# One lookup field's rows fetched by SyncE for every second tile instead of every third, with its row numbers on the chip, and the first gram portions ahead of two lookups

## What is computed

```python
e = jnp.stack([tbl_0[ids[:, 0]], ..., tbl_31[ids[:, 31]]], axis=1)      # [2048, 32, 256]
dots = jnp.einsum('bnd,bmd->bnm', e, e)
z = dots[:, iu, ju]                                                    # 496 pairs, i < j
h = jnp.concatenate([z, dense_ctx], axis=1)                            # 512 features
h = jnp.maximum(h @ W_top1 + b_top1, 0.0)                              # 512 -> 512
h = jnp.maximum(h @ W_top2 + b_top2, 0.0)                              # 512 -> 256
y = h @ W_top3                                                         # 256 -> 1
```

## Time and profile before

| | us |
|---|---|
| median of 3 runs (549.89 to 554.2) | 552.4 |
| profiled execution, its own time | 549.18 |
| its span, first to last instruction | 547.4 |

### The profile page before, as it was taken

The page is one execution under the profiler, slowest core; times in us unless marked ns, Lnnn a source line. Parts: engine busy times, 40 slices in busy tenths (PEclk is TensorE's granted clock), DMA queues, the critical chain, the costliest instruction groups (busy, mean ns, idle before and its releaser), DMA issues.

```text
span 547.4 us, 26273 instructions
## 1 busy us (share of the span) xinstructions
PE 502.7 (92%) x11015; PEld 463.4 (85%) x11015; DVE 249.3 (46%) x592; ACT 184.0 (34%) x355; POOL 393.2 (72%) x421
## 2 busy tenths in 40 slices
PE   0765899999999999999999999999899999989997
PEld 0764898999999989899888989989799998988986
DVE  3675462543536263343626435362633536253132
ACT  1786160522406051240605124060511505051152
POOL 6777767777777777777777777777777777777710
PEclk9997999999999999999999999999999999999999
DMA  8999544444444444444445444444444443443310
GB/s 198 263 262 311 146 117 121 120 120 130 120 120 128 120 121 125 120 118 128 118 121 129 122 118 119 130 120 118 127 121 118 118 125 118 116 116 109 111 32 2
DMA packets 38515, 71.10 MB, mean 130 GB/s; under 512 B 10942, under 2 KB 24638, under 8 KB 38398
## 3 DMA queue, kind: packets, MB, share of 16 engines
q0 software_dynamic: 19872, 54.29, 35.6%
q1 hardware_dynamic: 18526, 15.14, 11.3%
HBM read 69.39 MB, written 0.01 MB: 127 GB/s over the span
## 4 chain that ended last, share of the span: by engine, by line
PE 59%; POOL 22%; issue 9%; DMA 7%; DVE 2%; ACT 1%; POOLq 0%; DVEq 0%
PE look_ps L382 23%; POOL rows L336 22%; PE quad_ps L404 12%; PE top_ps L463 7%; DMA rows<-in_tbl,row_ids 6%; PE quad_ps L366 5%; PE turn_ps L366 5%; PE top_ps L484 4%; PE quad_ps L425 1%; PE top_ps L448 1%; DVE turned L689 1%; PE turn_ps L463 1%; ACT area L578 0%; DVE one_hot L761 0%; PE turn_ps L484 0%
## 5 line engine op out<-in xcount | busy, mean ns | idle before, releaser
L336 POOL DMA_INDIRECT rows<-in_tbl,row_ids x414 | 392.4, 948 | 128.4 <-issue 115.5
L382 PE MATMUL look_ps<-one_hot,small 125*128 125x256 f32 (+1 forms) x1536 | 220.3, 292 | 6.4 <-DVE small L751 6.2
L382 PEld LDWEIGHTS look_ps<-one_hot,small 125*128 125x128 f32 x1536 | 194.6, 192 | 9.8 <-issue 7.2
L761 DVE TENSOR_SCALAR one_hot<-ids_across,sub_row 125x256 fp32r<-125x256 int32 (+1 forms) x384 | 117.7, 378 | 119.9 <-PE look_ps L382 114.2
L404 PE MATMUL quad_ps<-turned 128*32 128x31 f32 x7680 | 103.8, 199 | 3.5 <-issue 2.5
L404 PEld LDWEIGHTS quad_ps<-turned 128*32 128x32 f32 x7680 | 85.7, 110 | 23.4 <-issue 4.5
L557 ACT ACTIVATE ahead<-look_ps 128x512 f32<-128x512 f32 (+1 forms) x48 | 28.0, 584 | 200.8 <-PE look_ps L382 200.4
L366 PE MATMUL turn_ps<-ident,rows 128*128 128x128 f32 x418 | 63.1, 281 | 23.4 <-DMA rows<-in_tbl,row_ids 21.2
L366 PEld LDWEIGHTS turn_ps<-ident,rows 128*128 128x128 f32 x418 | 46.5, 142 | 28.5 <-issue 15.0
L366 PE MATMUL quad_ps<-ident,rows 128*128 128x128 f32 x410 | 61.9, 281 | 7.1 <-DMA rows<-in_tbl,row_ids 5.8
L548 ACT ACTIVATE turned<-turn_ps 128x512 f32<-128x512 f32 x57 | 36.2, 635 | 64.2 <-PE quad_ps L404 44.8
(11 more groups left out here) (68 smaller groups left out, 196.0 us busy)
## 6 DMA issues: line engine op xcount, KB each, us to landing
area<-in_tbl SPq DMA_DIRECT2D x640, 1.0 KB
rows<-in_tbl,row_ids POOLq DMA_INDIRECT x414
ids_across<-in_small_ids SPq DMA_DIRECT2D x45, 128.0 KB, 3.5
landed<-in_tbl SPq DMA_DIRECT2D x6, 896.0 KB
w_sb<-in_W_top SPq DMA_DIRECT2D x4, 256.0 KB
landed<-in_tbl SPq DMA_DIRECT2D x6, 104.0 KB
w_sb<-in_W_top SPq DMA_DIRECT2D x1, 512.0 KB
area<-in_dense_ctx SPq DMA_DIRECT2D x16, 8.0 KB
```

What stands on the lines that cost most here:

```text
L336: pool.indirect_dma_start(out=rows[:, n % PLACES, j, :], out_offset=None, in_=tables[f], in_offset=bass.IndirectOffsetOnAxis(ap=row_ids[:, ...
L382: last = pe.matmul(look_ps[:, c * width:(c + 1) * width], small[:, f, r, part, c * P:(c + 1) * P], one_hot[n % 2][:, r, 0:width], start=(r ...
L761: last = dve.tensor_scalar(one_hot[n % 2][:, r, 0:width], ids_across[0:SP, n % IDS_RING, 0:width], sub_row[:, r:r + 1], None, ALU.is_equal)
```

## The change

Three things are changed.

1. `ROW_TILES` is now 3, 5, 7, 9, 11, 13 and 15: SP fetches field 31 for seven tiles in place of five, and POOL issues 412 gathers in place of 414. The eight groups for a tile are spread over two steps of SP's loop, four a step, after the first, the second and (two) the third list of ids.
2. The row numbers of these tiles (14 rows of 64) are copied once into a buffer on the chip, `row_list_sb`, and a group loads its 16 registers from there. The list of ids number 5 is loaded earlier.
3. In step 0 the gram portions 0 to 3 go ahead of lookup 4, which then runs in one piece; lookup 5 is cut into the last four portions (`first_look`).

```diff
-    ROW_EVERY = 3
-    ROW_TILES = list(range(ROW_EVERY, TILES, ROW_EVERY))
+    ROW_EVERY = 2
+    ROW_TILES = list(range(3, TILES, ROW_EVERY))
     ROWS_AT_ONCE = 16
     ROW_GROUPS = P // ROWS_AT_ONCE
-    GROUPS_AFTER = 3
+    GROUPS_AFTER = [1, 1, 2]
+    LISTED = P // 2
...
+        row_list_sb = sbuf("row_list_sb", [2 * len(ROW_TILES), LISTED], int32)
...
             def fetch_rows(i, group):
-                t = ROW_TILES[i]
                 if group == 0 and i > 0:
                     sp.wait_ge(turn_done, BEGIN[ROW_TILES[i - 1]] + ROW_UNIT + 1)
-                at = t * P + group * ROWS_AT_ONCE
+                if group == 0 and i == 0:
+                    sp.wait_ge(row_list_in, 16)
+                half, at = divmod(group * ROWS_AT_ONCE, LISTED)
                 _, numbers = nc.values_load_multi_w_load_instructions(
-                    row_list[0:1, at:at + ROWS_AT_ONCE], engines=[mybir.EngineType.SP],
+                    row_list_sb[2 * i + half:2 * i + half + 1, at:at + ROWS_AT_ONCE], engines=[mybir.EngineType.SP],
...
+            load_ids(5)
+            sp.dma_start(row_list_sb[:, :], row_list).then_inc(row_list_in, 16)
             load_dense(0)
...
-            load_ids(5)
             for t in range(TILES):
                 made = range(FIRST[t + 1], FIRST[t + 2]) if t + 2 in FIRST else range(0)
-                for k in range(GROUPS_AFTER):
+                begin = ROW_TILES[0] - ROW_EVERY
+                group = (t - begin) % ROW_EVERY * sum(GROUPS_AFTER)
+                for k, groups in enumerate(GROUPS_AFTER):
                     if k < len(made):
                         load_ids(made[k])
-                    group = t % ROW_EVERY * GROUPS_AFTER + k
-                    if t < ROW_TILES[-1] and group < ROW_GROUPS:
-                        fetch_rows(t // ROW_EVERY, group)
+                    if begin <= t < ROW_TILES[-1]:
+                        for _ in range(groups):
+                            fetch_rows((t - begin) // ROW_EVERY, group)
+                            group += 1
...
+            def first_look(k):
+
+                fifth, sixth = FIRST[0], FIRST[0] + 1
+                if k == PARTS // 2:
+                    look_up(fifth, 0, PRODUCTS)
+                if k > PARTS // 2:
+                    at = k - PARTS // 2 - 1
+                    look_up(sixth, PRODUCTS * at // (PARTS // 2), PRODUCTS * (at + 1) // (PARTS // 2))
...
                 for k in range(PARTS):
-                    look_between(t, k)
+                    if t > 0:
+                        look_between(t, k)
+                    else:
+                        first_look(k)
...
-                look_between(t, PARTS)
+                if t > 0:
+                    look_between(t, PARTS)
+                else:
+                    first_look(PARTS)
...
-    laid["row_list"] = np.ascontiguousarray(by_slot[:, FIELDS - 1].reshape(1, BATCH))
+    laid["row_list"] = np.ascontiguousarray(by_slot[:, FIELDS - 1].reshape(TILES, P)[3::2].reshape(-1, P // 2))
```

More of the change, by code:

```diff
@@ L189, in dlrm_tower @@
         table_in = [sem(f"table_in{i}") for i in range(SMALL)]
+        row_list_in = sem("row_list_in")
         rows_in = [sem(f"rows_in{i}") for i in range(len(ROW_TILES))]
```

## The result

The changed kernel takes 582.9 us (median of 4 runs, 580.91 to 584.57), the kernel before 551.75 in the same comparison: 5.8% slower, ratio 1.0576 with an interval of 1.054 to 1.0612. The forecast was 548.5, the range ended at 582.

The account below looks back on a forecast made before the run. POOL's gathers were taken as the bound; two gathers fewer (2.5 us) and step 0's new order (1.4) gave 3.9 us, SP's queue costing nothing, so 548.5 us from a median of 552.4, range 544 to 582.

Parts of the forecast that it names:

- What bounds the kernel: Whole span: POOL, one gather every 1.25 us, is the bound; PE keeps just ahead at 31.4 us a step.
- Part 1, two gathers fewer: POOL's queue: 412 gathers in place of 414 gain 2.5 us, with POOL staying the bound.
- Part 2, step 0: Start: gram portions ahead of lookup 4 let POOL's late gather at 73.05 go on time; gain 1.4 us.
- Part 3, SP's queue: SP's fetch of 128 rows every second tile: it fits POOL's 63.9 us with 1.8 us of room, costing nothing.
- the term x: SP's queue before each group: time of one register load from the buffer on the chip, taken as 0.6 us.
- The limit of 0.82 us: SP's load from the chip: below this time SP costs nothing against POOL's 63.9 us for two tiles.
- the period 57.3 + 8x: SP's cycle between last turns of its tiles: 57.3 us of issues and small terms plus eight loads; forecast 62.1.
- the prediction's formula: Span if SP decides: 138 to tile 3's last turn, six periods, 22.4 to the end; 504.2 + 48x.
- the 5.0 that the rivals' prices add: Whole kernel: medians taken as span plus 5.0 us, from 552.4 - 547.4 of the kernel before.
- a little too slow: Rival on SP's loads: x from 0.82 to 1.5, median 557 at 1.0 and 581 at 1.5; chance 0.17.
- The rule of a price for each register: SP's loads: about 200 ns per register from HBM; if true on chip, x 3.2, period 82.9, span 673.
- The floor of about 0.6 us for a load: SP's loads: skill's floor of about 600 ns for a tensor_load, cited for x = 0.6 and the period 62.1.

Follow-up runs that it names:

- load_once: The changed kernel with one load of 16 row numbers at the start, reused for every group (wrong rows fetched); 547.1 us, ratio 0.9911 to the kernel before.
- hbm_two: The changed kernel with SP's registers loaded from the list in HBM again, two loads a group; 698.8 us in one run.

## Why the prediction was wrong

**What bounds the kernel**: right. With SP out of the way (load_once) the gain was 0.9% where 0.7% was forecast, and POOL's last gather started at 519.1.

**Part 1, two gathers fewer**: 2.5 us were counted, and load_once with its 547.1 allows that and the gain of step 0 together. In the changed kernel they were worth nothing, since POOL waited some 30 us for PE.

**Part 2, step 0**: the mechanism was half right. The wait at lookup 4 went, and 4.5 us of stands in the middle of portion 2 and lookup 4 came for it. The step counted with portions of 0.8 us back to back, and nothing in its rows showed that PE would run through them without a stand. The kernel before already had such a stand of 1.36 us at 62.83 in its step 0, which I left out. The part by itself gave 0.5% in runs, more than the 1.4 us counted (0.25%). That it gave more is luck as far as the working goes: it was counted from a start with a mild wait of 1.68 us, and other starts of the old order have over 5.

**Part 3, SP's queue**: the sum was right and the term x was wrong. The limit of 0.82 us, the period 57.3 + 8x, the place of the wait (the last unit of every second tile), what is behind it, all came out. The step that failed is the choice x = 0.6 for the load: it measured 1.37. I took the pair of loads from HBM as two equal trips, of which the chip spares the whole, and left almost nothing for the 16 numbers. The runs show that most of the 1.37, 16 x 0.057 = 0.9, is paid by the number.

The prediction says that the pair doesn't tell whether 16 numbers cost more than one address. The gap doesn't, but the trace of the kernel before does, in the two rows of line 285 above: 1.17 us for the address and 1.83 for the 16 numbers. The trips were not equal, and the longer list cost 0.66 us more. An estimate from these rows alone, that this 0.66 stays and that SP's steps around the loads (the gap of at least 3.4 less 1.17 and 1.83, 0.4) stay too, is x = 1.06 before anything for the access on the chip. That is over the limit of 0.82, and by the prediction's own price the change would have been forecast as a small loss.

The other terms that were off by less:

- With x = 1.37 the prediction's formula gives a span of 504.2 + 48 x 1.37 = 570.0; measured were 581.1, which is 11.1 more. Tile 3's last turn was put at 138, and ended at 144.99: the first fetch began at 77.32 and not at 70, as PE's step 1 was not earlier, and was already SP-bound. That is 7.0 us.
- The period was 68.75 (from 144.99 to tile 15's 557.48) in place of 68.26, six times 0.5 = 2.9 us. It is the turn of the last unit, put at 0.4: behind PE's wait it takes 0.63 to 1.09 us, 0.93 in the mean of the six. From the turn's end to SP's first row DMA it is 1.36 us (144.99 to 146.35), the load and no more.
- The last gram products ran 8.90 us for 7.68 before, at a granted clock of 0.85 in place of 1.00, fallen after the last wait: 1.2 us.

```profile
558.17 8.90 PE L433 MATMUL quad_ps<-turned 128*64 128x62 f32 x256 [0.69 <-ACT turned L571]
```

The median lies 1.8 us above the span and not the 5.0 that the rivals' prices add: the profiled execution before was 3.2 us under its median, and the one after is the median itself. So the price in medians, 575, is 7.9 us short, while the span is 11.1 short.

**The rivals.** The time fell at the end of the rival that was called "a little too slow" (x from 0.82 to 1.5), which had 0.17. Its own price for x = 1.37 was 509.2 + 65.8 = 575, and the range ended at 582 because it ended at x = 1.5. That x lay inside this rival and the time just outside the range is the work of the three terms above.

The rule of a price for each register, from the Trainium skill ("Runtime: NRT & Kernel Launch", "Instruction fetch mechanics"), about 0.2 us each, was right in kind, since there is a price by the number, but not in size. The prediction has it agree with the pair's 3.4 to 4.0 us; this is chance. The 16 numbers from HBM take 1.83 us, 0.11 each, where the rule says 3.2, and the address takes 1.17, where it says 0.2 to 0.4. From the chip a number more costs 0.057. The floor of about 0.6 us for a load ("DMA: Bandwidth & Descriptors", "Latency and other measured facts", in the Trainium skill) is not contradicted, as the shortest load here took 0.69 with 8 numbers. But it is a floor, and it was taken for the whole load of 16.

**A version better than both.** Neither half of SP's change pays here; the order of step 0 alone does: 0.9952 (0.9931 to 0.9972), with the weights late 0.9946 (0.9927 to 0.9966). A second buffer for the fetched rows would take the landing and the turn out of SP's cycle. It doesn't fit: the on-chip memory is full to the last byte with the list of row numbers in it. So no run has it.

## What to carry to other kernels

When work is moved from a full queue to one that seems idle, write down the receiving queue's whole cycle from release to release and compare it with the period of its consumer: here the sum held within 1 us, and the decision hung on one unknown term with a room of 0.2 us. Before such a term is guessed from a gap, look for the instructions inside the gap: SP counts as never busy, but the view of the source line gave each load its time. Where the term has no row at all, the width of its possible values is the forecast; an optimistic value inside the room deserves less than an even chance. A register load with several numbers was priced here by a fixed part and a part for each number.

## What the runs showed of the hardware

- Loading n row numbers from a buffer on the chip into SP's registers holds SP's queue for 0.91, 1.37 and 2.27 us for 8, 16 and 32, that is 0.46 + 0.057 n. The instruction alone takes at least 0.69, 1.14 and 2.03 us.
- From HBM the load of 16 numbers takes 1.83 us and the load of the list's address 1.17 (medians of 40). The queue is held for 3.4 to 4.0 us by the pair where rows were shown, and for 3.0 to 4.8 in hbm_two.
- A one-row DMA of 1 KB with its address from a register takes SP 0.403 us (6.45 for 16), and 0.316 (5.05) where the same row numbers are used in every group.
- After waits of PE of 3 to 6 us its granted clock was lower for a while: 0.70 over layer 1 at tile 3, which took 5.22 us in place of 3.74 at 1.00.
- PE stands 2.4 to 4.0 us inside a run of small products, behind the 342nd product in all eight traces with the new order of step 0, and in six of them again 126 products later for 0.5 to 1.5 us. The profile names nothing; each time a packet of 16 KB of queue 8 (instruction) had ended 1.2 to 1.6 us before.
